# One core, a two-layer macaron block: 64 columns of a squaring step moved from GpSimd to VectorE in the second attention

## The reference

```python
S = jnp.einsum('bhnd,bhmd->bhnm', Q, K) / dh ** 0.5
W_tau = jax.nn.softmax(S, axis=-1)
W_sigma = 1.0 / ((1.0 + jnp.abs(S) / b_) ** 2 + t_ ** 2)
W_sigma = W_sigma / W_sigma.sum(axis=-1, keepdims=True)
tau = jnp.einsum('bhnm,bhmd->bhnd', W_tau, V)...
sigma = jnp.einsum('bhnm,bhmd->bhnd', W_sigma, V)...
f = 0.5 * tau + 0.5 * sigma
```

## Time and profile before

| | |
|---|---|
| median of 3 runs | 2976.28 us (2976.19 to 2976.68) |
| the profiled execution, its own time | 2972.06 us |
| its span in the trace | 2970.4 us |
| busy over the span | PE 2445.4 us, DVE 2491.1, ACT 2234.4, POOL 1992.1 |
| the second attention's squares | first at 1224.6 us, last ends at 2687.7 us |
| its instructions on POOL | L1761 256 x 3675 ns, L1758 256 x 1979 ns |
| its square on DVE | L1985 256 x 968 ns |

### The profile page before, as it was taken

How to read it: one execution, slowest core, us unless ns; L and a number is a source line. 1 busy time by engine, 2 the same in 40 slices (tenths; PEclk the granted TensorE clock), 3 DMA queues, 4 the chain that set the end, 5 groups by cost and what they waited for, 6 DMA issues and landing times. The chain is left out here.

```text
span 2970.4 us, 60006 instructions
## 1 busy us (share of the span) xinstructions
PE 2445.4 (82%) x18487; PEld 1018.8 (34%) x18614; DVE 2491.1 (84%) x3983; ACT 2234.4 (75%) x2441; POOL 1992.1 (67%) x1236
## 2 busy tenths in 40 slices
PE   3755999998577994689999999999999999983898
PEld 2642333333474662122222222222222222222566
DVE  4666888885577657799999999999999999996765
ACT  4532777777364543499999999999999999993554
POOL 4510222222453651499999999999999999994465
PEclk9976999999687997699999999999999999997799
DMA  3222111000120002000000000000000000000000
GB/s 116 70 64 87 30 29 29 28 27 11 45 79 5 1 0 86 22 15 14 16 15 14 14 16 15 14 14 16 15 14 14 16 15 14 14 5 0 1 12 18
DMA packets 93504, 76.58 MB, mean 26 GB/s; under 512 B 32480, under 2 KB 73960, under 8 KB 93264
## 3 DMA queue, kind: packets, MB, share of 16 engines
q1 hardware_dynamic: 89104, 66.36, 7.8%
q0 software_dynamic: 4288, 8.82, 0.9%
HBM read 47.77 MB, written 24.42 MB: 24 GB/s over the span
## 5 line engine op out<-in xcount | busy, mean ns | idle before, releaser
L1761 POOL TENSOR_TENSOR a_sg<-a_sg,all_f0w 128x1632 f32<-128x1632 f32 x256 | 940.7, 3675 | 21.3
L1967 DVE TENSOR_REDUCE a_mx<-a_pm 128x1 f32<-128x1024 f32 x512 | 618.3, 1208 | 23.2 <-PE a_pm L1813 23.2
L1978 DVE TENSOR_SCALAR a_sg<-a_pa 128x1024 int32<-128x1024 int32 x512 | 614.9, 1201 | 3.8 <-PE a_pa L1813 3.8
L1894 ACT ACTIVATE a_pt<-a_pb 128x1024 f32<-128x1024 f32 x512 | 532.4, 1040 | 55.0 <-PE a_pb L1813 53.4
L1831 PE MATMUL a_po<-a_pt,a_Vh 128*32 128x512 f32 x2048 | 538.4, 604 | 15.0 <-ACT a_osb L1913 11.4
L1831 PE MATMUL a_po<-a_sg,a_Vh 128*32 128x512 f32 x2048 | 538.3, 604 | 0.0
L1758 POOL TENSOR_SCALAR all_f0w<-a_sg,a_parh 128x1632 f32<-128x1632 f32 x256 | 506.7, 1979 | 37.4 <-DVE a_sg L1978 37.3
L1903 ACT ACTIVATE a_sg<-a_sg,a_parh 128x2048 f32<-128x2048 f32 x256 | 517.0, 2020 | 0.0
L1907 ACT ACTIVATE a_sg<-a_sg 128x2048 f32<-128x2048 f32 x256 | 496.0, 1937 | 0.0
L1581 ACT ACTIVATE a_pt<-a_ring 128x1024 f32<-128x1024 f32 (+2 forms) x384 | 313.7, 846 | 164.4 <-PE a_ring L1508 161.2
L1653 DVE TENSOR_REDUCE a_mx<-a_ring 128x2 f32<-128x1024 f32 (+3 forms) x384 | 359.2, 955 | 85.1 <-PE a_ring L1491 66.1
(11 more groups left out here) (265 smaller groups left out, 4457.9 us busy)
## 6 DMA issues: line engine op xcount, KB each, us to landing
all_Q<-q_parts SPq DMA_DIRECT2D x256, 48.0 KB
all_K<-k_parts SPq DMA_DIRECT2D x256, 48.0 KB
k_parts<-p_parts SPq DMA_DIRECT2D x16, 384.0 KB, 2.6
e_recs<-routed_rows SPq DMA_DIRECT2D x70, 64.5 KB, 1.9
n_xn<-expert_rows SPq DMA_DIRECT2D x16, 256.0 KB, 4.2
all_Q<-a_rows SPq DMA_DIRECT2D x256, 2.0 KB
q_parts<-p_parts SPq DMA_DIRECT2D x16, 192.0 KB, 2.3
q_parts<-p_parts SPq DMA_DIRECT2D x8, 384.0 KB, 2.6
```

The source lines that it names most:

```text
L1761: nc.gpsimd.tensor_tensor(buf[:, :, 0:CUT], buf[:, :, 0:CUT], sums, ALU.mult)\
L1894: nc.scalar.activation(pt[(j - LT) % 4][:, i, :], pb[:], ACT.Exp, scale=SC)\
L1967: nc.vector.tensor_reduce(mx[:, (j // PER) % 2, t:t + 1], pm[:], AX.X, ALU.max)\
L1978: nc.vector.tensor_scalar(sg[(j - LS) % 4][:, i, :].bitcast(I32), pa[:].bitcast(I32), SIGN_OFF, None, ALU.bitwise_and).then_inc(abs_done, 1)
```

## The change

The number that splits the square goes from 51/64 to 49/64 of a tile:

```diff
     SC = DH ** -0.5
-    CUT = 51 * T // 64
+    CUT = 49 * T // 64
     WIDE = TT * (DH + 1)
```

## The result

The changed kernel takes 2954.94 us, the median of 4 runs (2953.90 to 2956.16); the kernel before, run again beside it, 2976.24 us (2970.76 to 2976.68, 4 runs). The ratio is 0.9933, with a 95% interval of 0.9916 to 0.9950: faster by 21.3 us on the medians, by some 15 to 25 us within the interval. The two profiled executions are 2972.06 and 2955.36 us, 16.7 us apart.

What follows compares the result with a forecast made beforehand. POOL with DVE's square in its cycle was taken as the bound at 22.855 us a head, then ACT at 22.48: 0.375 x 57.5 = 21.5 us saved, 2976.28 - 21.5 = 2954.8 us; range 2949 to 2974.

Steps and rivals of the forecast that it cites:

- What bounds the kernel before: Second attention: POOL, with DVE's square inside its cycle, sets the pace at 22.85 us a head; ACT is next.
- The three terms: Per slot: L1761 shorter by 0.142 us, L1758 shorter by 0.058, DVE's square longer by 0.065 while POOL stands.
- The pair's head: POOL and DVE after the change: the longer of the two in each of four slots, together 22.40 us a head.
- ACT as the bound: After the change ACT loses its one wait a head and sets the pace at 22.48 us; chance 0.55.
- longer instructions on ACT: Sign against the prediction: it falls if ACT's instructions get longer; no size given.
- A: Rival: POOL and DVE stay the bound at 22.69 us a head, gain 9.5 us, 2966.8 us; chance 0.20.
- B: Rival: ACT's wait moves to another pb in PE's queue, gain under 6 us, some 2973 us; chance 0.13.
- C: Slower rival: L1758 starts before DVE's square, which waits; 23.75 us a head, 3027 us; chance 0.12 including similar turns.
- The lead of 0.12 us: In the earlier trace DVE's square started 0.12 us before POOL's L1758 and won the turn.

Runs made afterwards that it cites:

- experiment 5: Kernel before, with ScalarE's second exponential over 960 of a tile's 1024 columns: 2973.28 us, 1.6 us under the kernel before beside it.
- 2: Kernel before, with VectorE's square at 240 columns a tile in place of 208, GpSimd keeping 816: 2988.29 us, 13.3 us more than the kernel before.
- 8: Kernel before, with VectorE's square cut to 8 columns a tile, 200 left unsquared, GpSimd's share as before: 2955.57 us.
- experiment 6: Changed kernel, with ScalarE's second exponential over 960 of a tile's 1024 columns: 2951.70 us.
- 1: Changed kernel, with VectorE's square back at its old 208 columns a tile, 32 left unsquared: 2958.30 us.
- 4: Changed kernel, with the split moved one more step, 752 columns a tile with GpSimd: 2954.71 us, 0.9932 of before.

## Why the prediction was right, and where it was off

*What bounds the kernel before.* Right. The pair of POOL and DVE, taking turns, set the pace: a shorter ACT queue changed nothing (experiment 5), a longer square on DVE cost its full 0.066 us a slot though DVE had time (2), and a square taken away gave the gain (8). The page of the Trainium skill that the prediction names for the turn, "SBUF — State Buffer", section "Who interferes with whom", says that a VectorE instruction with two SBUF inputs contends with a GpSimd instruction that reads SBUF. Experiments 2 and 8 agree with it from both sides: 64 more columns of the square made GpSimd's L1758 0.067 us longer, and with almost no square it was 0.33 us shorter.

*The three terms.* L1761 fell by 0.141 us (0.142 taken). L1758's end behind the square fell from 1.49 to 1.44 us (0.058 taken, 0.05 measured). The unhindered square rose from 0.65 to 0.72 us (0.065 taken), so of the two ends, 0.065 and 0.100, the one by the step between two widths was right. POOL's slot came to 5.56 us, 5.555 was worked out.

*The pair's head.* It was put at 22.40 us and is 22.49 (6). Half of the missing 0.09 us is DVE's longest slot: 5.655 us was worked out from one head with 4.94 us between two squares, and 4.94 is the shortest that occurs; the distance goes from there to some 5.06 us and is 4.98 on average, before the change as in experiment 6. Most of the rest is the slot with L1956, 5.64 us in experiment 6 and not 5.605.

*ACT as the bound.* Right: three kernels with a pair that is faster by very different amounts (1, 4 and 8) all stay at 22.54 to 22.57 us, and only a shorter ACT queue (6) goes below. The term that was off is ACT's own head. 22.48 us was read from the starts of the earlier trace rows, just where ACT had stopped waiting and its rows began to grow; by the ends of the same two rows it is 22.56, and in the changed kernel 22.55. That start to start is the better measure of what an instruction costs its engine, as was said ahead of the prediction, holds where the engine comes to a stop once a head; for ACT without a wait it was 0.07 us a head short. So 0.315 us a head was saved and not 0.375, 18 us and not 21.5. The prediction had named longer instructions on ACT as a sign against it. The rows did get longer, L1894 from 1.02 to 1.41 us and more, but the ends didn't move apart by it.

*The time.* 2954.8 us was predicted and 2954.94 measured, but agreement as close as that is luck. The stage gave 18.3 us of the 21.5. The medians differ by 3 us more than that, the two profiled executions by 1.6 us less; both lie within the interval of the ratio. The profiled execution itself was put at 2950.6 us and took 2955.36.

*The rivals.* A, the pair as the bound at 22.69 us, fell: 22.49, hidden behind ACT by 0.05. B, the wait that moves within PE's queue, cost nothing: the wait behind the four transposes went, and the start that is now 0.05 us late, behind the weighing that waits for the copy, leaves ACT's ends where they were. C did not occur, though POOL was idle or just done when both engines went for the same data. One such place, a square of DVE:

```profile
1406.77 0.72 DVE L1985 SCALAR_TENSOR_TENSOR a_sg<-a_sg,a_parh 128x480 f32<-128x480 f32 x1
```

and the L1758 beside it:

```profile
1406.80 2.05 POOL L1758 TENSOR_SCALAR all_f0w<-a_sg,a_parh 128x1568 f32<-128x1568 f32 x1
```

The square started 0.03 us earlier, had its unhindered 0.72 us, and L1758 ended 1.36 us later, at 1408.85. The lead of 0.12 us that the prediction saw in the earlier trace rows was thus not needed, and no square of the middle of the stage took longer than 1.01 us. In each of the 256 slots the square's row starts before that of its L1758; the other order, which C needs, did not come up, and no run shows what it would cost.

## What to carry to other kernels

When two engines take turns, the row of each one holds the other's work: subtract it (here by the distance between their ends) before a share of the work is moved, and count the hold on both sides. A move between two engines gains only down to the next full queue, so read that queue's own cycle first; one step past it (47/64) costs nothing here and brings nothing. And read that cycle from row end to row end, over several heads: when an engine has just been freed of a wait, its starts can run ahead, here for six heads, and make it look faster than it is.

## What was not expected of the hardware

ACT's rows get longer when its queue never runs dry: the copy went from 0.62 to 1.01 us within six heads and no further, and L1894 shows 1.02 us in the earlier trace rows and 1.41 to 1.45 us in the changed kernel, with 0.90 us to the next start in both (2008.07 to 2008.97). The engine isn't slower for it, since the ends stay 22.55 us a head apart. But who needs the result gets it with the end of the row: PE's weighing starts 0.05 to 0.15 us behind the end of the copy, whether that row is short or long. So neither the duration of such a row nor the distance between starts is its price; the distance between ends is.
